# A four-layer graph network on one core: a turned copy of x for the first layer, its projections ahead of its aggregation, its bias added by DMA, loads in another order

## What is computed

```python
def _L0_gnn_ref(H, adj, W, b):                       # 8 heads of 32, together 256
    H_ = jnp.einsum('nd,hde->hne', H, W)
    out = jnp.einsum('nm,hme->hne', adj, H_) + b[:, None, :]
    return jnp.transpose(out, (1, 0, 2)).reshape(H.shape[0], HEADS * DPH)
...
x = _layernorm(x + _L0_gnn_ref(x, adj, L0_gnn_W, L0_gnn_b), axis=-1)
x = _layernorm(x + _L1_gnn_ref(x, adj, L1_gnn_W, L1_gnn_a), axis=-1)   # attention, 4 heads
x = _layernorm(x + _L2_gnn_ref(x, adj, ...), axis=-1)                  # two graph convolutions
x = _layernorm(x + _L3_gnn_ref(x, adj, L3_gnn_W), axis=-1)             # adj + I, normalised by degree
```

## Time and profile before

| what | value |
|---|---|
| median of three runs | 712.02 us (711.02 to 712.37) |
| the profiled execution | 711.94 us, its span 710.2 us |
| PE busy | 690.8 us (97%) |
| DVE, ACT, POOL busy | 529.1, 402.7, 142.9 us |
| moved by DMA | 40.09 MB |
| chain that ended last | PE 86%, DVE 9% |

### The profile page before, as it was taken

One profiled execution on the slowest core, in us unless ns is written; L12 is line 12 of the kernel. 1 busy time (PEld: TensorE's weight loads), 2 busy tenths in 40 slices (PEclk: granted clock), 3 DMA queues, 4 the chain that ended last, 5 costly groups with the idle time before them and its releaser, 6 DMA issues.

```text
span 710.2 us, 16787 instructions
## 1 busy us (share of the span) xinstructions
PE 690.8 (97%) x6026; PEld 570.9 (80%) x6026; DVE 529.1 (75%) x991; ACT 402.7 (57%) x541; POOL 142.9 (20%) x233
## 2 busy tenths in 40 slices
PE   5989999999999999999999999999999999999996
PEld 4878854688888888888888888866677778888885
DVE  4888646999898989989898998997343325874564
ACT  6555146888989889798888979644300021123000
POOL 3966422000100000000000001622021112332222
PEclk9999999999999999999999999999999999999999
DMA  8976001000313021030301203000021000110011
GB/s 325 411 292 270 0 3 59 1 1 30 61 31 60 1 59 30 30 59 30 59 0 36 52 0 60 1 1 1 1 45 24 15 1 16 39 30 1 30 46 45
DMA packets 24445, 40.09 MB, mean 56 GB/s; under 512 B 13073, under 2 KB 19153, under 8 KB 22225
## 3 DMA queue, kind: packets, MB, share of 16 engines
q1 hardware_dynamic: 21824, 31.63, 13.0%
q0 software_dynamic: 2016, 7.34, 5.5%
q10 hardware_dynamic: 560, 0.52, 0.2%
HBM read 27.13 MB, written 2.13 MB: 41 GB/s over the span
## 4 chain that ended last, share of the span: by engine, by line
PE 86%; DVE 9%; DMA 1%; ACT 1%; issue 1%; POOL 1%; SPq 0%; DVEq 0%; POOLq 0%; ACTq 0%
PE ps L520 15%; PE ps L521 15%; PE ps L661 14%; PE ps L663 14%; PE ps L662 14%; PE ps L511 8%; PE ps L611 5%; DVE ring_hl L954 2%; DVE ring_a L949 2%; PE ps L478 1%; DMA x<-in_x 1%; DVE x L729 1%; DVE stat L723 1%; POOL ring_a L1086 0%; DVE x L983 0%
## 5 line engine op out<-in xcount | busy, mean ns | idle before, releaser
L663 PE MATMUL ps<-arena,ring_hl 128*128 (+1 forms) x1024 | 279.6, 273 | 0.0
L661 PE MATMUL ps<-arena,ring_hl 128*128 (+1 forms) x1024 | 278.8, 272 | 0.4 <-DVE ring_hl L954 0.4
L662 PE MATMUL ps<-arena,ring_hl 128*128 (+1 forms) x1024 | 278.6, 272 | 0.0
L520 PE MATMUL ps<-arena,adj 128*128 128x256 f16 (+1 forms) x1024 | 230.3, 272 | 0.5 <-issue 0.5
L521 PE MATMUL ps<-arena,adj 128*128 128x256 f16 x1024 | 230.4, 273 | 0.0
L949 DVE SCALAR_TENSOR_TENSOR ring_a<-rho,gam,ring_a 128x1024 f32<-128x1024 f32 x128 | 163.9, 1281 | 18.0 <-ACT ring_a L412 18.0
L426 ACT ACTIVATE ring_hl<-ring_a 128x1024 f16<-128x1024 f32 x128 | 135.2, 1056 | 45.2 <-PE ps L663 31.0
L954 DVE TENSOR_TENSOR ring_hl<-ring_a,ring_hl 128x1024 f16<-128x1024 f32 x128 | 156.1, 1220 | 6.0 <-ACT ring_hl L426 5.9
L412 ACT ACTIVATE ring_a<-adj,shift 128x1024 f32<-128x1024 bf16 x128 | 145.5, 1138 | 0.0
L520 PEld LDWEIGHTS ps<-arena,adj 128*128 (+1 forms) x1024 | 99.9, 98 | 17.8 <-issue 0.9
L521 PEld LDWEIGHTS ps<-arena,adj 128*128 (+1 forms) x1024 | 99.5, 97 | 15.6
(11 more groups left out here) (91 smaller groups left out, 576.3 us busy)
## 6 DMA issues: line engine op xcount, KB each, us to landing
arena<-in_adj SPq DMA_DIRECT2D x16, 1024.0 KB, 8.6
x<-y POOLq DMA_DIRECT2D x14, 512.0 KB, 5.2
rho<-s_scratch SPq DMA_DIRECT2D x8, 512.0 KB, 3.7
out_x<-x SPq DMA_DIRECT2D x16, 128.0 KB, 1.7
x<-in_x SPq DMA_DIRECT2D x3, 512.0 KB, 7.6
arena<-in_L_gnn_W SPq DMA_DIRECT2D x1, 1024.0 KB, 16.4
arena<-in_L_gnn_a SPq DMA_DIRECT2D x1, 1024.0 KB, 18.4
rho<-in_L_gnn_W SPq DMA_DIRECT2D x2, 512.0 KB, 9.4
```

The costliest lines, as they stand in the source:

```text
L520: nc.tensor.matmul(ps[:, bank, 0:width], lhs, pp[:, j, 0, 0:width], start=(j == 0), stop=False)
L661: nc.tensor.matmul(acc, hi, v_hi, start=(jt == 0), stop=False)
L662: nc.tensor.matmul(ps[:, b, 0:D], hi, v_lo, start=False, stop=False)
L663: ins = nc.tensor.matmul(acc, lo, v_hi, start=False, stop=(jt == T - 1))
```

## The change

The host makes two more things: `x_turned`, x laid out `[128, 16 tiles, 256]` with features on the partitions as the projection wants it, and the bias repeated four times. In the kernel:

- x turned is loaded first, in five transfers, to `xts`, the arena's words that `w1` and `a` use later. x itself is loaded in four transfers of 0.5 MB: the first behind pieces 0 to 3 of adj, the others behind pieces 4 to 7 and 8, 9. `w1` and `a` are loaded when all of x turned has been split (SP waits for `s_lo` = 16).
- ACT writes `hi` of x turned in pieces of two tiles, DVE the `lo` of tiles 0 and 1, POOL that of the others (128 x 512 each). There are no transposes and no `take_t` in the first layer.
- PE runs 28 matmuls of zeros first (`WARM`), then all 16 projections (now in four PSUM banks), then the whole of `group0` for tiles 0 to 3.
- The bias is added to x by four accumulating DMAs of 0.5 MB that POOL issues: the first behind its splits, the others behind its work for normalised tiles 1, 2 and 3. DVE's `first` of tiles 0, 4, 8, 12 waits for them.
- The eight products for `W` times `a` are shared: four on POOL, four on DVE; the last pair stands behind the statistics of tile 0.
- The order of DVE's `fill` is another: cast 8 moves from tile 2's place to tile 5's, and the splits of `w1`, `w2a`, `w2b`, `w3` move later. On ACT the casts and weight copies move too.

```diff
@@ SP
-            sp.dma_start(x[:, 0, :], xr[:, 0, :]).then_inc(ld_x[0], 16)
+            sp.dma_start(xts[:, 0, :], xt_in[:, 0, :]).then_inc(ld_xt[0], 16)
             for r in range(R):
                 first = max(r * R, 1)
-                sp.dma_start(x[:, first:(r + 1) * R, :], xr[:, first:(r + 1) * R, :]).then_inc(ld_x[r + 1], 16)
-            sp.dma_start(bias0, b0_in.rearrange("(a n) -> a n", a=1).partition_broadcast(P)).then_inc(ld_b, 16)
+                sp.dma_start(xts[:, first:(r + 1) * R, :], xt_in[:, first:(r + 1) * R, :]).then_inc(ld_xt[r + 1], 16)
...
             for n in FIRST_LOADS:
                 load_adj(n)
+            load_x(0)
+            sp.wait_ge(s_lo, T)
             sp.dma_start(w1f, w1_in.rearrange("(k p) (h f) -> p k h f", p=P, h=H)).then_inc(ld_w1, 16)
...
-            load_adj(STAGES)
-            load_adj(STAGES + 1)
+            for n in range(STAGES, 2 * STAGES):
+                load_adj(n)
+            load_x(1)
+            load_adj(2 * STAGES)
+            load_adj(2 * STAGES + 1)
+            load_x(2)
+            load_x(3)
+            load_adj(2 * STAGES + 2)
+            load_adj(2 * STAGES + 3)
@@ PE
+            pe.wait_ge(s_warm, 1)
+            for _ in range(WARM):
+                nc.tensor.matmul(ps[:, 0, 0:P], warm, warm, start=True, stop=True)
...
-            joint(0, 0, lambda t: 2 * (t + 1 - T) + T - 1, columns_cast)
+            for t in range(T):
+                project(0, t, t % R)
+            for j in range(T):
+                columns_cast(j)
+                group0(0, 0, [j])
@@ DVE
+            def products(n):
+
+                heads = slice(2 * (n % 2), 2 * (n % 2) + 2)
+                if n == 1:
+                    dve.wait_ge(ld_w1, 16)
+                    dve.wait_ge(ld_a, 16)
+                else:
+                    dve.wait_ge(s_wa, n - 2)
+                nc.vector.tensor_tensor(prod[:, heads], w1f[:, n // 4, heads], abc[:, heads, n // 2 % 2, :], ALU.mult)\
+                  .then_inc(s_prod_dve, 1)
+                sum_products(n)
+                sum_products(n - 1)
...
+            for t in range(T):
+                take(0, t, t % R)
+                if t == 9:
+                    cast_n(0)
+                if t == 12:
+                    cast_n(2)
+            cast_n(1)
+            cast_n(3)
+            products(1)
+            products(3)
+            cast_n(4)
+            products(5)
...
-            fill = {0: was_lo, 1: lambda: weight_lo(3, w2b, w2bf), 2: lambda: cast_n(8),
-                    3: lambda: weight_lo(4, w3, w3f), 4: lambda: cast_n(10), 5: lambda: weight_lo(1, w1, w1ff),
-                    6: lambda: cast_n(12), 7: lambda: cast_n(14)}
+            fill = {0: lambda: products(7), 1: was_lo, 2: lambda: cast_n(6), 3: lambda: None,
+                    4: lambda: weight_lo(1, w1, w1ff), 5: lambda: cast_n(8), 6: lambda: None, 7: lambda: cast_n(10),
+                    8: lambda: weight_lo(2, w2a, w2af), 9: lambda: cast_n(12), 10: lambda: weight_lo(3, w2b, w2bf),
+                    11: lambda: (cast_n(14), weight_lo(4, w3, w3f))}
@@ POOL
-            def add_b0(t, u):
-                pool.wait_ge(s_lo, t + 1)
-                nc.gpsimd.tensor_tensor(tile_of(x, t), tile_of(x, t), bias0, ALU.add).then_inc(s_xb, 1)
-            tiles(pool, 0, T, add_b0)
+            for lo, hi in CHUNKS[2:]:
+                pool.wait_ge(s_hi, hi)
+                nc.gpsimd.tensor_sub(xt[:, lo:hi, D:2 * D], xts[:, lo:hi, :], xt[:, lo:hi, 0:D]).then_inc(s_lo, hi - lo)
+
+            def add_b0(r):
+                pool.wait_ge(ld_x[r], 16)
+                nc.gpsimd.dma_start(x[:, r * R:(r + 1) * R, :].rearrange("p t d -> p (t d)"),
+                                    b0_in.rearrange("(a n) -> a n", a=1).partition_broadcast(P), accum_op=ALU.add)\
+                  .then_inc(s_xb[r], 16)
+            add_b0(0)
...
+            for t in range(R):
+                norm_and_lo(t, t)
+                if t > 0:
+                    add_b0(t)
+            tiles(pool, R, T, norm_and_lo)
```

159 lines of the change are left out of this document (90 added, 69 removed).

## The result

The changed kernel is slower: 716.63 us (median of 7 runs, 715.58 to 717.87) against 712.37 (7 runs, 711.02 to 713.88), ratio 1.0063 [1.0049, 1.0077]: 0.6%, small but clear of the noise. Its profiled execution has a span of 714.9 us, against 710.2. The forecast was 709.1. Its range ended at 713.3.

What follows compares the result with a forecast made beforehand. PE's matmuls bound the kernel, so early gains reach the end: -7.4 (joint aggregation) + 1.1 (products) - 1.3 (transpose) + 0.2 (cast 6) + 4.4 (cast 8) = -3.0, giving 709.1 us; range 705 to 713.3.

Steps and rivals of the forecast that it cites:

- Joint aggregation: First layer, tiles 0 to 3: without transposes, paced by POOL's splits, PE leaves it at 33.3 us, 7.4 earlier.
- fourth rival: First-layer projections: PE stays at the low clock, 1.3 us each, giving 715; chance 0.07.
- E is pushed by 0 to 1.9 us; I take 1.1: E, PE leaving the joint aggregation: late `w1`, `a` and products delay the first sum, moving E to 34.4.
- S: Mark when PE starts output tile 8: forecast 55.7 us against 58.6 before, -2.9 us.
- From the first sum to the first transpose: Ahead of the next layer's first transpose: 5.6 us in place of 6.9, a gain of 1.3 us.
- Cast 8: Output tile 8: DVE's cast of piece 8, behind the sum of tile 4, makes PE wait 4.4 us.
- round-robin rule: Second bias DMA: engines alternate between queues with work, so 2.6 us of moving become 5.2, S 2 us later.
- The second: Rival: loads of x come too late, holding POOL's third bias DMA and tile 4's sum; +3, 715; chance 0.18.
- The third: Rival: products and bias each at their worse end, so no change, 712; counted in the forecast's worse tail.

Runs made afterwards that it cites:

- run 7: Changed kernel without the 28 warming matmuls (`WARM = 0`): 716.25 us.
- Run 2: Changed kernel with matmuls of zeros in PE's two long waits, 90 ahead of tile 4 and 70 ahead of tile 8: 714.51 us.
- run 12: Kernel before the change with two unused 1 MB loads, one ahead of the adj pieces, one behind piece 5: 715.71 us.
- run 13: As run 11, with cast 3 ahead of products(3), casts 10, 12, 14 one place earlier, POOL's bias additions singly for tiles 4 to 6: 715.00 us.
- 5: Changed kernel without the products of `w1` and `a`, these loaded behind pieces 4 to 7, small weights zeros: 715.85 us.
- 6: Changed kernel with products(5) on DVE behind the first sums instead of ahead of them: 715.79 us.
- 10: Changed kernel with the bias added by POOL instead of accumulating DMAs, and cast 8 back at tile 3's place: 716.81 us.
- run 11: Changed kernel with bias added by POOL, cast 8 early, `w1` and `a` loaded and products done early, weight copy ahead of cast 7: 714.76 us.
- run 1: Changed kernel with DVE's cast of piece 8 moved from tile 5's place to tile 3's: 713.48 us.
- run 4: Changed kernel without the bias transfers for tiles 4 to 15 (three of four accumulating DMAs): 710.24 us.
- 9: Changed kernel with the bias added by POOL in sixteen additions instead of the accumulating DMAs: 716.62 us.
- 3: Changed kernel with x turned staged in `adj`'s last columns, and `w1`, `a` loaded behind pieces 0 and 2: 717.00 us.
- 8: Changed kernel with x turned in `adj`, loads ordered 0, 2, x, `w1`, `a`, 1, 3, products ahead of cast 4, cast 8 early: 716.00 us.
- 16: Changed kernel with the bias of all 16 tiles added by 64-row matmuls on PE, and the products early: 711.96 us.
- Run 18: Changed kernel with bias on PE by 128-row matmuls, products early, 60 matmuls of zeros ahead of source tile 8: 708.14 us.
- 17: Changed kernel with bias of tiles 4 to 15 by 64-row matmuls on PE, plus 90 matmuls of zeros before tile 4: 712.62 us.

## Why the prediction was wrong

**Joint aggregation: right.** 33.3 forecast, 32.8 measured, within the 1 to 2 us by which executions differ there; POOL's pieces paced the projections, its last one 15.14 to 17.08 (forecast 17.6). The slow projections of the fourth rival lasted to about 8.8 us and stayed hidden behind POOL, as the prediction had it for that case, and the warming had no part in it (run 7). Its reason against the rival was misread: PE had not been without a gap for 6 us in the kernel before (0.89 us of idle time ahead of 9.46).

**The step that failed first: "E is pushed by 0 to 1.9 us; I take 1.1".** It was 5.4. Two parts of it were too small. I had `w1` and `a` at 24.6, "27.2 at worst", from bytes divided by the rate. `a` came at 28.6, 11 us after its issue, beside pieces 4 to 7, which were issued right behind it (18.0 to 22.1). And the work from there to the first sum took 9.0 us, not 7.0 to 7.5: a pair of products takes 2.45, with POOL's multiplication 1.64 to 2.18 beside DVE against 1.26 in the earlier trace rows, and the third pair has a DVE multiplication of 1.75 beside POOL's.

**What the sum left out: the clock behind a wait.** I weighed the low clock for the projections alone, as the fourth rival; behind a wait I put it at nothing, without a reason. It came behind each of the two long waits, with 2.4 and 2.6 us. Run 2 measures what that costs in the end: all of the second, 0.5 of the first, since DVE was late behind it anyway. The Trainium skill's rule in "TensorE: Matmul & The Clock Gate", section "HAM oscillation — how this bites in real kernels", that a PE which idles comes back cold, agrees with these rows. The length of the idle time does not settle it in all of them. Behind the sixteen waits of 4.3 us or more that PE has in these traces between 25 and 110 us, the matmuls were slow each time. Behind shorter ones they were in some cases (2.26 us in run 12, 2.27 in run 13, 3.1 in runs 5, 6 and 10) and not in others (2.26 in the kernel before, 2.6 and 3.1 in run 11, 3.0 and 3.5 in run 1). What decides there stays open.

**In numbers.** The span missed its forecast by 7.6 us (714.9 for 707.3): 3.8 by tile 4's start (5.4 for 1.1, less 0.5 of the joint aggregation), 1.8 between that and S, 2.0 behind S.

**From the first sum to the first transpose: right in kind.** Without the clock it is 4.4 us where I took 5.6.

**Cast 8: the wait was right, 4.4 forecast and 4.4 measured, but that both ends moved by the same amount is luck.** I had the sum of tile 4 14.3 us behind tile 4's start, waiting for POOL; it was 16.3, waiting for the bias DMA, which was issued 7.2 us behind tile 4's start (I had 8.5) and landed 9.1 us behind its issue, where I took the 5.2 of a quiet queue. PE was late itself by 1.8 us more than I had it behind the same mark (the clock's 2.4, the 0.65, less the quicker transpose), so the difference stayed. The Trainium skill's round-robin rule in "DMA: Bandwidth & Descriptors", section "Queues, rings and completion order", which I had set beside this step, would have put the landing 7.8 us behind the issue, by my estimate; the trace goes the same way and further.

**Rivals.** The second (x late) was near but did not happen: x landed at 48.2 to 49.0, where its own sum had 47.8, and POOL came at 49.0. (The loads that this sum names add up to 16.5 MB, not 17.7.) Run 5 uncovered it. The third, products and bias both at their worse end, was nearest in kind. It ended at 712, since the first sum came 3.0 us later than its worse end (37.7 for 34.7) and the clock was not in it.

**Where the gain of the design went.** It had two mendable parts. Leaving the late bias out gives 6.4 us (run 4), and the same work on POOL takes it all back (9, 13); on PE with 128 rows it costs 0.1 us a tile. The products' place costs up to 5.4 and a clock of 2.4 behind it. Mending it makes PE wait for pieces 1 and 3 in the joint aggregation, by 0.7 to 6.2 us (3, 8, 11, 13, 16), partly because the loads of `w1` and `a` now stand in front of them (8, 13; run 12 has the price of such bytes), partly because DVE does products ahead of the cast (11, 16). Run 18 takes both parts, fills the wait for piece 3, and keeps 3.6 us.

## What to carry to other kernels

When work is taken off the critical engine, list what the next marks need from each other engine and when it lands. A sum that gains 7 us on PE moves every wait that was hidden by these 7 us into view, one behind the other, and taking away a single one can show nothing (run 5) or half of what it was thought to cost (runs 1 and 2). A load that is issued into a full queue is not priced by its bytes at the full rate: bound it by the longest issue-to-landing time of a row from the busiest stage. An idle time of PE of 4 us or more should be priced with the low clock behind it, 2.4 to 2.6 us here; where the wait can't be removed, matmuls of zeros kept the clock in runs 2, 17 and 18.
